# Expert outputs in one PSUM bank instead of two, and a bank of their own for the turned sums of the gathered groups

## The chip, the cores and the metric

One Trainium2 chip, one core of it. The metric is the device time of one launch in microseconds (us), as the median of several runs; lower is better. The engines are TensorE (PE; its weight loads are shown apart as PEld), VectorE (DVE), ScalarE (ACT), GpSimd (POOL) and SyncE (SP, which here only starts DMAs).

## What is computed

Two layers on a tensor x of 4 x 32 x 32 tokens with 128 channels, all in float32. Cut to what matters:

```python
x = x + L0_conv(ln(x))      # deformable convolution: 8 groups of 32 channels, 9 points each,
                            # each point read bilinearly (4 corners) at a place that depends on the token
t = t + L0_ffn(ln(t))       # 8 experts, one per token: y = relu(x @ w1[e] + b1[e]) @ w2[e] + b2[e],
                            # times the probability of the expert, 0 if the expert is over capacity
x = x + L1_conv(ln(x))      # attention in a 7 x 7 window, 8 heads of 16 channels
t = t + L1_ffn(ln(t))       # 8 experts again
```

## The kernel before

The 4096 tokens are 32 tiles of 128. The work on one tile i is a "slot" (function `slot`), in two halves: `beside_second` runs beside the eight experts of the second layer for tile i - 4, `beside_first` beside the eight experts of the first layer for tile i - 1. Each half is one "pass" of `experts`, numbered u. Slots 4 to 22 and 23 to 29 are two hardware loops; slots 0 to 3, 30 and 31 are written out. Behind slot 31 (`final=True`) come five passes (`beside_0` to `beside_4`) that finish the last tiles. There is no scheduler: every engine runs the same order of parts, written by hand, and they wait for one another by semaphores (`Steps`: `step` names what an instruction completes, `done` is the value to wait for).

**Experts.** In a pass, PE multiplies `up(e)` into bank `Z[e % 2]` (L1581, 4 products), ACT makes `hid` of it (L1404), and PE multiplies `down(e)` into `Y[e // 4]` (L1591, 4 products), a quarter bank for each expert. The order on PE is up(e + 1), the early parts of `beside(e)`, down(e), the other parts of `beside(e)`. DVE weights and sums the outputs in `add_up` (L1201): experts 0 to 3 at e = 4, behind `beside(4)` (steps `a0` to `a3`), experts 4 to 7 in `close` (`a4` to `a7`), which stands in `beside(0)` of the next pass; then the rest of `close` adds the result to X. So `down(0)` of a pass waits for `a3` of the pass before, and `down(4)` for `a7` of the pass before. `a0` needs also `share` (the bias part, product L1569, copied by ACT in L1396).

**The convolution.** Six of the eight groups are gathered: POOL starts 54 indirect DMAs for a tile (L894, nine for each group q, into `got[:, q]`), DVE multiplies the weights in (`conv("mix")`, L1130), PE turns and sums the nine points (`conv("gather")`, L1533) and ACT copies the sum to `mixed_T` (L1375). The other two groups are made without a gather: DVE makes 16 masks a tile (`dense("make")`, L1053, called m0 to m15 here), PE turns and sums each (`dense("sum")`, L1490) and ACT copies two at a time to `spread` (L1339). Both kinds of sum go to bank `DGB`: the dense ones to its columns 0 to 255, the gathered ones to columns 256 to 383. The waits keep the engines apart by bank: a gathered sum waits for the copy of the dense ones and of the gathered one before, and a dense sum behind a gathered one for its copy (`freed=mixed`).

POOL writes `got[:, q]` for tile t again when PE has turned it for tile t - 1; in `flow(s)`, s = 0 to 15 of a slot, the parts above are spread over its sixteen experts (`MIXED` says at which s a group is mixed).

Of the kernel before, what the change touches and what calls it, by code (L numbers as in the profile page):

```python
# [36 lines left out]
P = 128  # L37
# [87 lines left out]
def build(nc, x, v_w, v_b, qd_w, qd_b, qs_w, qw_w, qw_b, out_w, out_b, prior, dscale,  # L125
# [3 lines left out]
    with ctx:  # L129
# [6 lines left out]
        def bank(name):  # L136
            return ctx.enter_context(nc.psum_tensor(name, [P, 512], F32))
# [108 lines left out]


        Z = [bank("Z0"), bank("Z1")]
        Y = [bank("Y0"), bank("Y1")]
        N = [bank("N0"), bank("N1")]  # L250
        DGB = bank("DGB")
        CV = bank("CV")
        ALL = [*Z, *Y, *N, DGB, CV]


        x_in = [sem(f"x_in{part}") for part in range(2)]
# [59 lines left out]
        def slots(eng, conv, route, experts, close, qkv, attend, values, places, dense):  # L316


            def slot(i, u1, u0, u0_before, ends, qk, att, e1, val=True, place=True, final=False):
# [4 lines left out]
                at = MIXED if not final else (1, 4, 6, 9, 11, 13)  # L324

                def flow(s):
                    mixed = (conv_s.done(f"c{NQ - 1}", i - 1) if s == 0 else
                             conv_s.done(f"c{at.index(s - 2)}", i) if s - 2 in at else None)
                    if s == 2:
                        dense("apart", i, 1)  # L330
                    if s == 3:
                        dense("now", i, None, i + TB - 1 if val else last)
                    if s == 5:
                        dense("weigh", i, 1)
                    if s == 10 and not final:
                        dense("apart", i + 1, 0)
                    if s == 13 and not final:
                        dense("weigh", i + 1, 0)
                    if s in at:
                        conv("mix", i, at.index(s))  # L340
                    if final and 7 <= s <= 10:
                        dense("make", i, 2 * s - 6)
                        dense("make", i, 2 * s - 5)
                    elif s < 15 and not (final and s > 10):
                        dense("make", i, s + 1)
                    elif not final:
                        dense("make", i + 1, 0)
                    if s - 1 in at:
                        conv("gather", i, at.index(s - 1), (s if s <= 8 else min(16, 2 * s - 8)) if final else s)
                    if final and 8 <= s <= 11:  # L350
                        dense("sum", i, 2 * s - 8, mixed)
                        dense("sum", i, 2 * s - 7)
                        dense("copy", i, s - 4)
                    elif s < 8 or not final:
                        dense("sum", i, s, mixed)
                        if s % 2:
                            dense("copy", i, s // 2)
                    if s - 1 in at:
                        conv("copy", i, at.index(s - 1), (s if s < 8 else min(15, 2 * s - 7)) if final else s)
# [186 lines left out]
            def beside_0(e, early):  # L546
                if early:
# [15 lines left out]
                        route("share", 1, last - 3)  # L563
                    return
                if e == 0:
                    route("pick", 0, last)
                    route("exp", 0, last)
                    close(u - 1, 0, last - 1)
                if e == 1:
                    route("pick", 1, last - 3)  # L570
                    route("exp", 1, last - 3)
# [341 lines left out]
        def _(v):  # L913
# [271 lines left out]
            def add_up(u, n, t, e0, e1):  # L1185

                d, s = exp_v.done, exp_v.step
                gate = route_b[n][:, 5, :]

                v.wait_ge(*exp_t.done(f"y{e1 - 1}", u))  # L1190
                for e in range(e0, e1):
                    so_far = acc
                    if e == 0:

                        v.wait_ge(*route_v[n].done("gate", t))
                        v.wait_ge(*route_s[n].done("b2", t))
                        v.wait_ge(*exp_v.all(u - 1))
                        so_far = share[n]
                    else:
                        v.wait_ge(*d(f"a{e - 1}", u))  # L1200
                    v.scalar_tensor_tensor(out=acc[:, :], in0=Y[e // 4][:, (e % 4) * D:(e % 4 + 1) * D],  # L1201
                                           scalar=gate[:, e:e + 1], in1=so_far[:, :],
                                           op0=ALU.mult, op1=ALU.add).then_inc(*s(f"a{e}"))

            def experts(u, n, t, beside):
                for e in range(E):
                    beside(e, True)
                    beside(e, False)
                    if e == 4:
                        add_up(u, n, t, 0, 4)  # L1210

            def close(u, n, t):
                d, s = exp_v.done, exp_v.step
# [95 lines left out]
        def _(a):  # L1309
# [59 lines left out]
            def conv(part, t, q=None, mine=None):  # L1369
                if part == "copy":  # L1370

                    a.wait_ge(*conv_t.done(f"g{q}", t))
                    a.wait_ge(*dense_t.done(f"k{mine}", t))
                    a.wait_ge(*conv_t.done("proj", t - 1))
                    a.activation(mixed_T[:, q, :], DGB[:, 2 * P:3 * P], ACT.Copy).then_inc(*conv_s.step(f"c{q}"))  # L1375

            def route(part, n, t, freed=None, held=None, placed=None):
                s = route_s[n].step
# [70 lines left out]
        def _(pe):  # L1449
# [29 lines left out]
            def dense(part, t, n=None, freed=None):  # L1479
                if part == "sum":  # L1480
                    pe.wait_ge(*dense_v.done(f"m{n}", t))

                    if n >= 2:
                        pe.wait_ge(*dense_s.done(f"s{n // 2 - 1}", t))
                    else:
                        pe.wait_ge(*dense_s.done("s7", t - 1))
                    if freed is not None:
                        pe.wait_ge(*freed)
                    for k in range(K):
                        ins = pe.matmul(DGB[:, n % 2 * P:(n % 2 + 1) * P], made[:, n % MADE, k * P:(k + 1) * P],  # L1490
                                        ident[:, :], is_transpose=True, start=(k == 0), stop=(k == K - 1))
                    ins.then_inc(*dense_t.step(f"k{n}"))
# [32 lines left out]
            def conv(part, t, q=None, mine=None):  # L1525
                s = conv_t.step
                if part == "gather":
                    pe.wait_ge(*conv_v.done(f"m{q}", t))

                    pe.wait_ge(*(conv_s.done(f"c{q - 1}", t) if q else conv_s.done(f"c{NQ - 1}", t - 1)))  # L1530
                    pe.wait_ge(*(dense_s.done(f"s{mine // 2 - 1}", t) if mine > 1 else dense_s.done("s7", t - 1)))
                    for k in range(K):
                        ins = pe.matmul(DGB[:, 2 * P:3 * P], got[:, q, k * PATCH:(k + 1) * PATCH], ident[:, :],  # L1533
                                        is_transpose=True, start=(k == 0), stop=(k == K - 1))
                    ins.then_inc(*s(f"g{q}"))
                if part == "project":
# [35 lines left out]
            def experts(u, n, t, beside):  # L1572
# [11 lines left out]

                def down(e):
                    pe.wait_ge(*exp_s.done(f"h{e}", u))
                    if e % 4 == 0:

                        pe.wait_ge(*exp_v.done(f"a{e + 3}", u - 1))
                    for c in range(FC):  # L1590
                        ins = pe.matmul(Y[e // 4][:, (e % 4) * D:(e % 4 + 1) * D], hid[:, e % 2, c, :],  # L1591
                                        w2[n][:, e * FC + c, :], start=(c == 0), stop=(c == FC - 1))
                    ins.then_inc(*s(f"y{e}"))

# [124 lines left out]
```

## Time and profile before

| | before |
|---|---|
| time, median of 3 runs | 2698.65 us (2695.47 to 2699.51) |
| time of the profiled execution | 2693.5 us |
| its span, first to last instruction | 2691.7 us |
| PE busy | 2315.7 us (86%) |
| DVE busy | 1912.4 us (71%) |
| ACT busy | 1221.7 us (45%) |
| POOL busy | 1941.1 us (72%) |
| mean granted clock of PE | 0.938 of full speed |

The table says how long an engine worked, not what sets the end. For that one reads the chain that ended last, then the time line of a tile in the loop and that of the end of the program, where POOL has no more gathers.

### The profile page before, as it was taken

How to read it: one execution, taken by the hardware profiler on the slowest of the kernel's cores; microseconds unless marked ns; L12 is line 12 of the kernel's file. 1: busy time of each engine (PE TensorE's matmuls, PEld its weight loads, DVE VectorE, ACT ScalarE, POOL GpSimd, SP SyncE). 2: the span in 40 equal slices, each digit the busy share in tenths (PEclk: the TensorE clock that was granted, in tenths of full speed). 3: DMA queues.
4: the chain of work that ended last, by engine and by line, in shares of the span. 5: the costliest groups of instructions: out<-in, count | busy, mean ns of one | idle time of the engine just before them, and what ended most of it. 6: DMA issues, size and time to landing. Idle time of an engine off the chain costs nothing.

```text
span 2691.7 us, 61285 instructions
## 1 busy us (share of the span) xinstructions
PE 2315.7 (86%) x18976; PEld 2202.2 (82%) x18976; DVE 1912.4 (71%) x4404; ACT 1221.7 (45%) x3974; POOL 1941.1 (72%) x1797
## 2 busy tenths in 40 slices
PE   1477689999988999999999999898988988898988
PEld 1466688988888898888889888888988888898887
DVE  4566677777777777777777777777777777776643
ACT  1123345544544554454455445445544544554455
POOL 3777777777777777777777777777777777777600
PEclk6788899999999999999999999999999999999989
DMA  9512212222221222222122222212111111111100
GB/s 190 140 50 54 60 55 57 57 59 59 60 58 54 57 55 59 59 60 60 54 56 54 59 59 60 60 54 56 48 54 53 54 52 53 49 50 54 49 16 10
DMA packets 219754, 158.70 MB, mean 59 GB/s; under 512 B 149530, under 2 KB 186988, under 8 KB 219596
## 3 DMA queue, kind: packets, MB, share of 16 engines
q0 software_dynamic: 55296, 113.36, 14.8%
q1 hardware_dynamic: 164300, 43.73, 7.4%
q14 instruction: 119, 0.97, 0.1%
q8 instruction: 39, 0.64, 0.1%
HBM read 138.90 MB, written 18.04 MB: 58 GB/s over the span
## 4 chain that ended last, share of the span: by engine, by line
POOL 68%; issue 22%; PE 5%; DVE 1%; ACT 1%; POOLq 1%; SPq 1%; DMA 1%; ACTq 0%; DVEq 0%
POOL got L894 68%; PE Y L1591 1%; PE Z L1581 1%; SPq L760 1%; POOL ranks L886 1%; ACT hid L1404 0%; PE N L1634 0%; PE DGB L1533 0%; PE N L1660 0%; ACT prob L1433 0%; PE N L1652 0%; DMA got<-patches,ranks 0%; PE DGB L1490 0%; DVE made L1053 0%; DVE acc L1201 0%
## 5 line engine op out<-in xcount | busy, mean ns | idle before, releaser
L894 POOL DMA_INDIRECT got<-patches,ranks x1728 | 1925.0, 1114 | 565.7 <-issue 507.8
L1404 ACT ACTIVATE hid<-Z,b 128x128 f32<-128x128 f32 x2048 | 575.3, 371 | 439.4 <-PE Z L1581 439.1
L1053 DVE TENSOR_TENSOR made<-tent 128x1152 f32<-128x1152 f32 x512 | 690.9, 1351 | 9.7 <-PE DGB L1490 9.4
L1490 PE MATMUL DGB<-ident,made 128*128 128x128 f32 x4608 | 611.6, 280 | 54.5 <-DVE bias L1118 39.8
L1591 PE MATMUL Y<-w,hid 128*128 128x128 f32 x4096 | 591.4, 290 | 22.7 <-ACT hid L1404 15.2
L1490 PEld LDWEIGHTS DGB<-ident,made 128*128 128x128 f32 x4608 | 540.1, 146 | 68.8 <-DVE bias L1118 40.6
L1591 PEld LDWEIGHTS Y<-w,hid 128*128 128x128 f32 x4096 | 526.0, 200 | 58.3 <-issue 26.5
L1581 PE MATMUL Z<-xt_m,w 128*128 128x128 f32 x4096 | 536.4, 277 | 0.5 <-ACT xt_m L1386 0.5
L1581 PEld LDWEIGHTS Z<-xt_m,w 128*128 128x128 f32 x4096 | 494.9, 193 | 6.9 <-issue 6.6
L1130 DVE TENSOR_TENSOR got<-got,wq 128x1152 f32<-128x1152 f32 x192 | 260.4, 1356 | 193.1 <-DMA got<-patches,ranks 186.8
L1339 ACT ACTIVATE spread<-DGB 128x256 f32<-128x256 f32 x256 | 97.6, 381 | 463.3 <-PE DGB L1490 460.2
L1533 PE MATMUL DGB<-ident,got 128*128 128x128 f32 x1728 | 251.3, 297 | 25.4 <-DVE got L1130 24.7
L1533 PEld LDWEIGHTS DGB<-ident,got 128*128 128x128 f32 x1728 | 221.0, 155 | 32.1 <-DVE got L1130 27.0
L1201 DVE SCALAR_TENSOR_TENSOR acc<-Y,route,acc 128x128 f32<-128x128 f32 x448 | 156.7, 350 | 76.9 <-issue 57.8
L1565 PE MATMUL CV<-ident,route 128*8 128x128 f32 x128 | 30.8, 333 | 168.5 <-DVE route L1183 168.5
L1565 PEld LDWEIGHTS CV<-ident,route 128*8 128x8 f32 x128 | 6.3, 88 | 182.1 <-DVE route L1183 181.4
L1500 PE MATMUL N<-spread,v_now 128*32 128x128 f32 x1024 | 123.4, 274 | 14.7 <-ACT spread L1339 14.7
L1500 PEld LDWEIGHTS N<-spread,v_now 128*32 128x32 f32 x1024 | 106.4, 110 | 26.5 <-ACT spread L1339 22.5
L1433 ACT ACTIVATE prob<-prob,soft 128x100 f32<-128x100 f32 x256 | 93.2, 373 | 0.0
L1393 ACT ACTIVATE gate_T<-CV 8x128 f32<-8x128 f32 x64 | 16.5, 258 | 156.3 <-PE CV L1565 156.1
L1381 ACT ACT_TABLE_LOAD x62 | 79.5, 1283 | 1.1
L1389 ACT ACT_TABLE_LOAD x61 | 78.3, 1283 | 1.1
(185 smaller groups left out, 2319.8 us busy)
## 6 DMA issues: line engine op xcount, KB each, us to landing
got<-patches,ranks POOLq DMA_INDIRECT x1728
vwin<-vpad SPq DMA_DIRECT2D x320, 40.0 KB
patches<-arena SPq DMA_DIRECT2D x92, 96.0 KB
w<-in_L_ffn_w SPq DMA_DIRECT2D x2, 2048.0 KB
patches<-got SPq DMA_DIRECT2D x38, 96.0 KB, 3.0
vpad<-vt SPq DMA_DIRECT2D x128, 16.0 KB
out<-X SPq DMA_DIRECT2D x32, 64.0 KB, 1.6
X<-in_x SPq DMA_DIRECT2D x1, 576.0 KB, 4.6
```

The costliest lines, as they stand in the source:

```text
L894: pool.indirect_dma_start(out=got[:, q, j * PATCH:(j + 1) * PATCH], out_offset=None, in_=table, in_offset=bass.IndirectOffsetOnAxis(ap=ran ...
L1053: v.tensor_tensor(made[:, n % MADE, :].rearrange("p (k y x) -> p k y x", k=K, y=CHUNK), tent[g][:, 1, :, c * CHUNK:(c + 1) * CHUNK].unsque ...
L1130: v.tensor_tensor(g3, g3, wj.unsqueeze(2).to_broadcast([P, QJ * CORNERS, C]), ALU.mult)\
L1201: v.scalar_tensor_tensor(out=acc[:, :], in0=Y[e // 4][:, (e % 4) * D:(e % 4 + 1) * D], scalar=gate[:, e:e + 1], in1=so_far[:, :], op0=ALU. ...
L1339: a.activation(spread[:, 2 * n:2 * n + 2, :].rearrange("p c q -> p (c q)"), DGB[:, 0:2 * P], ACT.Copy).then_inc(*dense_s.step(f"s{n}"))
L1404: ins = a.activation(hid[:, e % 2, c, :], Z[e % 2][:, c * P:(c + 1) * P], ACT.Relu, bias=b1[n][:, e * FC + c:e * FC + c + 1])
L1433: ins = a.activation(prob[:, j, :], prob[:, j, :], ACT.Exp, bias=soft[:, 1, j:j + 1], accum_out=soft[:, 2, j:j + 1])
L1490: ins = pe.matmul(DGB[:, n % 2 * P:(n % 2 + 1) * P], made[:, n % MADE, k * P:(k + 1) * P], ident[:, :], is_transpose=True, start=(k == 0), ...
L1500: ins = pe.matmul(N[1][n * C:(n + 1) * C, 0:P], v_now[:, c, n * C:(n + 1) * C], spread[:, n * CHUNKS + c, :], start=(c == 0), stop=(c == C ...
L1533: ins = pe.matmul(DGB[:, 2 * P:3 * P], got[:, q, k * PATCH:(k + 1) * PATCH], ident[:, :], is_transpose=True, start=(k == 0), stop=(k == K ...
L1581: ins = pe.matmul(Z[e % 2][:, c * P:(c + 1) * P], w1[n][:, e, c * P:(c + 1) * P], xt_m[n][:, :], start=True, stop=True)
L1591: ins = pe.matmul(Y[e // 4][:, (e % 4) * D:(e % 4 + 1) * D], hid[:, e % 2, c, :], w2[n][:, e * FC + c, :], start=(c == 0), stop=(c == FC - 1))
```

## The change

The outputs of all eight experts share one bank `Y`, in two rounds of four. `down(0)` waits for `a7` of the pass before and the new wait of `down(4)` is for `a3` of its own pass. DVE's first `add_up` of a pass stands ahead of `beside(4)` instead of behind it, and in `beside_0` `close` stands ahead of `pick` and `exp`. The bank that is free becomes `GS`, with a quarter of it for each gathered sum in turn; the waits between the gathered and the dense sums are left out.

```diff
-        Y = [bank("Y0"), bank("Y1")]
+        Y = bank("Y")
+        GS = bank("GS")
...
                 def flow(s):
-                    mixed = (conv_s.done(f"c{NQ - 1}", i - 1) if s == 0 else
-                             conv_s.done(f"c{at.index(s - 2)}", i) if s - 2 in at else None)
...
-                        dense("sum", i, s, mixed)
+                        dense("sum", i, s)
...
                 if e == 0:
+                    close(u - 1, 0, last - 1)
                     route("pick", 0, last)
                     route("exp", 0, last)
-                    close(u - 1, 0, last - 1)
...
-                    v.scalar_tensor_tensor(out=acc[:, :], in0=Y[e // 4][:, (e % 4) * D:(e % 4 + 1) * D],
+                    v.scalar_tensor_tensor(out=acc[:, :], in0=Y[:, (e % 4) * D:(e % 4 + 1) * D],
...
             def experts(u, n, t, beside):
                 for e in range(E):
+                    if e == 4:
+                        add_up(u, n, t, 0, 4)
                     beside(e, True)
                     beside(e, False)
-                    if e == 4:
-                        add_up(u, n, t, 0, 4)
...
                     a.wait_ge(*conv_t.done(f"g{q}", t))
-                    a.wait_ge(*dense_t.done(f"k{mine}", t))
                     a.wait_ge(*conv_t.done("proj", t - 1))
-                    a.activation(mixed_T[:, q, :], DGB[:, 2 * P:3 * P], ACT.Copy).then_inc(*conv_s.step(f"c{q}"))
+                    a.activation(mixed_T[:, q, :], GS[:, q % 4 * P:(q % 4 + 1) * P], ACT.Copy).then_inc(*conv_s.step(f"c{q}"))
...
-                    if freed is not None:
-                        pe.wait_ge(*freed)
...
-                    pe.wait_ge(*(dense_s.done(f"s{mine // 2 - 1}", t) if mine > 1 else dense_s.done("s7", t - 1)))
                     for k in range(K):
-                        ins = pe.matmul(DGB[:, 2 * P:3 * P], got[:, q, k * PATCH:(k + 1) * PATCH], ident[:, :],
+                        ins = pe.matmul(GS[:, q % 4 * P:(q % 4 + 1) * P], got[:, q, k * PATCH:(k + 1) * PATCH], ident[:, :],
...
                 def down(e):
                     pe.wait_ge(*exp_s.done(f"h{e}", u))
-                    if e % 4 == 0:
-
-                        pe.wait_ge(*exp_v.done(f"a{e + 3}", u - 1))
+                    if e == 0:
+                        pe.wait_ge(*exp_v.done("a7", u - 1))
+                    if e == 4:
+                        pe.wait_ge(*exp_v.done("a3", u))
```

On DVE, in the first loop at e = 4 of a slot's first half, there stands before (from m4 on; the first row made is m4, the second m5; `route` holds the gates, and rows of ISA and REGISTER_ALU are waits and addresses):

```order
L1053 TENSOR_TENSOR made<-tent 128x1152
L1130 ISA
L1130 TENSOR_TENSOR got<-got,wq 128x1152
L1049 REGISTER_ALU
L1053 TENSOR_TENSOR made<-tent 128x1152
L1190 ISA
L1195 REGISTER_ALU
L1196 REGISTER_ALU
L1201 SCALAR_TENSOR_TENSOR acc<-Y,route,share 128x128
...
L1160 TENSOR_TENSOR route<-CV,gb 128x8
```

and now, one line number lower:

```order
L1052 TENSOR_TENSOR made<-tent 128x1152
L1189 ISA
L1194 REGISTER_ALU
L1195 REGISTER_ALU
L1200 SCALAR_TENSOR_TENSOR acc<-Y,route,share 128x128
...
L1129 ISA
L1129 TENSOR_TENSOR got<-got,wq 128x1152
L1048 REGISTER_ALU
L1052 TENSOR_TENSOR made<-tent 128x1152
L1158 REGISTER_ALU
L1159 TENSOR_TENSOR route<-CV,gb 128x8
```

The four sums (three of them left out in the rows) have moved ahead of the mix of group 1 and of m5; the rest of the slot keeps its order.

On DVE, at e = 4 of the first pass behind the last slot (`beside_0`), there stands before (QT, KT and vt are the attention's queries, keys and values, `turns` the spread queries):

```order
L1250 TENSOR_SCALAR xn_q<-X,mv_q,rs_q 128x128
L1256 TENSOR_SCALAR QT<-N,bq 128x4x8x4
L1260 TENSOR_SCALAR KT<-N,bq 128x4x32
L1265 TENSOR_TENSOR vt<-N,bv 128x128
L1201 SCALAR_TENSOR_TENSOR acc<-Y,route,share 128x128
L1201 SCALAR_TENSOR_TENSOR acc<-Y,route,acc 128x128 x3
```

and now:

```order
L1249 TENSOR_SCALAR xn_q<-X,mv_q,rs_q 128x128
L1200 SCALAR_TENSOR_TENSOR acc<-Y,route,share 128x128
L1200 SCALAR_TENSOR_TENSOR acc<-Y,route,acc 128x128 x3
L1255 TENSOR_SCALAR QT<-N,bq 128x4x8x4
L1259 TENSOR_SCALAR KT<-N,bq 128x4x32
L1264 TENSOR_TENSOR vt<-N,bv 128x128
```

The sums have moved ahead of the three parts of the attention, and are no longer between these and the spread queries (L1271 before).

## Rows read from the trace of the kernel before

**Rows 1.** The page: POOL in 40 slices of the span; the chain, shares by engine.

```profile
POOL 3777777777777777777777777777777777777600
...
POOL 68%; issue 22%; PE 5%; DVE 1%; ACT 1%; POOLq 1%; SPq 1%; DMA 1%; ACTq 0%; DVEq 0%
```

**Rows 2.** Groups of instructions, one tile of the loop (1183 to 1262 us): busy, mean; idle before.

```profile
L894 POOL DMA_INDIRECT got<-patches,ranks x54 | 60.4, 1118 | 17.7 <-issue 15.9 <-POOL ranks L886 1.8
```

**Rows 3.** Waits over the whole span: total us, times, longest us.

```profile
PE DGB L1490 <- ACT mixed_T L1375: 8.8, 15, 1.6
```

**Rows 4.** Time line of POOL in that tile: start, duration, instruction, idle before.

```profile
1238.15 1.82 POOL L894 DMA_INDIRECT got<-patches,ranks  x1 [0.31 <-issue]
1240.28 0.96 POOL L894 DMA_INDIRECT got<-patches,ranks  x1 [0.30 <-issue]
...
1246.56 1.65 POOL L894 DMA_INDIRECT got<-patches,ranks  x1 [0.30 <-issue]
```

**Rows 5.** Time line of DVE in that tile: a7, m4, mix, pick, m6.

```profile
1222.22 1.51 DVE L1201 SCALAR_TENSOR_TENSOR acc<-Y,route,acc 128x128 f32<-128x128 f32 x4 [3.04 <-issue]
...
1237.80 1.35 DVE L1053 TENSOR_TENSOR made<-tent 128x1152 f32<-128x1152 f32 x1
1239.07 1.35 DVE L1130 TENSOR_TENSOR got<-got,wq 128x1152 f32<-128x1152 f32 x1
...
1243.75 0.17 DVE L1160 TENSOR_TENSOR route<-CV,gb 128x8 f32<-128x8 f32 x1 [0.64 <-PE CV L1556]
...
1246.04 1.35 DVE L1053 TENSOR_TENSOR made<-tent 128x1152 f32<-128x1152 f32 x1
```

**Rows 6.** Time line of PE in that tile: down(0), down(3), down(4), the long wait.

```profile
1224.48 1.15 PE L1591 MATMUL Y<-w,hid 128*128 128x128 f32 x8 [0.39 <-DVE fin L1223]
...
1237.57 1.16 PE L1591 MATMUL Y<-w,hid 128*128 128x128 f32 x8
...
1240.55 1.06 PE L1591 MATMUL Y<-w,hid 128*128 128x128 f32 x8
...
1254.56 0.59 PE L1565 MATMUL CV<-ident,route 128*8 128x128 f32 x2 [4.01 <-DVE route L1183]
```

**Rows 7.** Time line of PE at the end: down(0) and down(4) of slot 31's second pass.

```profile
2519.49 1.16 PE L1591 MATMUL Y<-w,hid 128*128 128x128 f32 x8
...
2537.91 1.06 PE L1591 MATMUL Y<-w,hid 128*128 128x128 f32 x8
```

**Rows 8.** Time line of DVE there: a4 to a7, then a1 to a3.

```profile
2519.80 1.50 DVE L1201 SCALAR_TENSOR_TENSOR acc<-Y,route,acc 128x128 f32<-128x128 f32 x4
...
2539.15 1.12 DVE L1201 SCALAR_TENSOR_TENSOR acc<-Y,route,acc 128x128 f32<-128x128 f32 x3
```

**Rows 9.** Time line of PE, passes one to three and five behind slot 31.

```profile
2570.59 1.16 PE L1591 MATMUL Y<-w,hid 128*128 128x128 f32 x8
...
2576.53 2.67 PE L1634 MATMUL N<-KT,turns 128*128 128x100 f32 x16 [1.88 <-DVE turns L1271]
...
2587.80 1.95 PE L1591 MATMUL Y<-w,hid 128*128 128x128 f32 x8 [2.04 <-ACT hid L1404]
...
2601.86 1.06 PE L1591 MATMUL Y<-w,hid 128*128 128x128 f32 x8
...
2618.58 2.00 PE L1591 MATMUL Y<-w,hid 128*128 128x128 f32 x8 [2.92 <-ACT hid L1404]
...
2680.33 1.06 PE L1591 MATMUL Y<-w,hid 128*128 128x128 f32 x8
```

**Rows 10.** Time line of ACT in pass one: the copy of share.

```profile
2571.30 0.29 ACT L1396 ACTIVATE share<-CV 128x128 f32<-128x128 f32 x1
```

**Rows 11.** Time line of DVE: a4 to a7 in passes two and three, a1 to a3 in pass five.

```profile
2587.75 1.50 DVE L1201 SCALAR_TENSOR_TENSOR acc<-Y,route,acc 128x128 f32<-128x128 f32 x4
...
2618.41 1.50 DVE L1201 SCALAR_TENSOR_TENSOR acc<-Y,route,acc 128x128 f32<-128x128 f32 x4
...
2680.03 1.12 DVE L1201 SCALAR_TENSOR_TENSOR acc<-Y,route,acc 128x128 f32<-128x128 f32 x3
```

More of the change, by code:

```diff
@@ L252, in build @@
         CV = bank("CV")
-        ALL = [*Z, *Y, *N, DGB, CV]
+        ALL = [*Z, Y, GS, *N, DGB, CV]
         x_in = [sem(f"x_in{part}") for part in range(2)]
@@ L350, in flow @@
                     if final and 8 <= s <= 11:
-                        dense("sum", i, 2 * s - 8, mixed)
+                        dense("sum", i, 2 * s - 8)
                         dense("sum", i, 2 * s - 7)
@@ L1586, in down @@
                     pe.wait_ge(*exp_s.done(f"h{e}", u))
-                    if e % 4 == 0:
-                        pe.wait_ge(*exp_v.done(f"a{e + 3}", u - 1))
+                    if e == 0:
+                        pe.wait_ge(*exp_v.done("a7", u - 1))
+                    if e == 4:
+                        pe.wait_ge(*exp_v.done("a3", u))
                     for c in range(FC):
-                        ins = pe.matmul(Y[e // 4][:, (e % 4) * D:(e % 4 + 1) * D], hid[:, e % 2, c, :],
+                        ins = pe.matmul(Y[:, (e % 4) * D:(e % 4 + 1) * D], hid[:, e % 2, c, :],
                                         w2[n][:, e * FC + c, :], start=(c == 0), stop=(c == FC - 1))
```

## The prediction

> **What bounds the kernel now.** I read the page first. The chain that ended last lies on POOL for 68% of the span and in the gaps between its calls for 22%; in the slices POOL works through 38 of 40 and is idle in the last two [rows 1]. The groups of one tile of the loop say what a call costs: 54 calls with 60.4 us busy and 17.7 between them, 78.1 us for a tile, and none of the 17.7 is a wait for PE [rows 2]. PE waits 4.01 us in one place of that tile, for a gate that DVE makes only after it has waited for gathered data [rows 6]: PE has some 4 us to spare in each tile. So in the loop an edit counts only if it makes the 54 calls longer, or costs PE more than that reserve. Behind the gathers, POOL's last two slices, PE, ACT and DVE set the end, and there each new wait of PE counts.
>
> A call is not always the same length: 0.96 us or 1.82 or 1.65 [rows 4]. Laid beside DVE's time line, the long ones started while DVE worked on m4 or m6 (1237.80 to 1239.15 and 1246.04 to 1247.39), and both ended 0.82 us after that product's end [rows 4, 5]. A call that starts under such a mask product is held to its end. The first lost 0.86 us by that, the second 0.69.
>
> **Part 1, the sums in a bank of their own.** It removes waits between PE and ACT and adds no instruction: the same products and copies, other columns. The largest of these waits as the trace names them, of PE for a copy to mixed_T, is 8.8 us in the whole span, 15 times [rows 3]. Most of it lies before POOL's end, inside the reserve. Taken as 0; bounds 0 and -1 us.
>
> **Part 2, one Y bank, in the loop.** down(0) now waits for a7 of the pass before. In the tile shown a7 is done at 1222.22 + 1.51 = 1223.73 and down(0) starts at 1224.48 [rows 5, 6]: 0.75 us to spare, no wait. down(4) waits for a3 of its own pass. The output of expert 3 is there at 1237.57 + 1.16 = 1238.73, DVE is free behind m4 at 1239.07, four sums take 1.5 us: a3 at 1240.57, and down(4) started at 1240.55 [rows 5, 6, 11]. PE thus waits some 0.05 us, and I allow as much again for weights that are not loaded ahead. The logits behind it and DVE's pick, which already waits for them (0.64 us), come that much later, m6 too, and with m6 the end of the call held under it. That is 0.1 us a tile on POOL's own time, for 32 tiles +3 us. Bounds: 0, if the wait stays hidden, and +6 with as much in the tile's other pass.
>
> **Part 3, the moved sums.** The mix of group 1 and m5 start 1.5 us later and fill time in which DVE waited for the logits: 1240.57 + 2 x 1.27 = 1243.1, before 1243.75 [rows 5]. (1.27 is the distance from m4 to the mix.) Which call is held changes. The call at 1240.28 no longer meets the mix; the one 1.25 us later starts at 1241.5 under it and is held to 1241.8, some 0.25 us; every later call shifts by that, so the call under m6 starts 0.25 later and is held 0.25 less, 0.45 in place of 0.69. The sum for the tile stays: 0. Had one call more or less fitted between m4 and m6, it would be another sum (below).
>
> The Trainium skill, "SBUF — State Buffer", section "Who interferes with whom", says that a tensor_tensor has no two-port mode, contends only with GpSimd's reads and did not stall the writing of descriptors. The calls of [rows 4] beside [rows 5] speak against this for indirect DMAs. By the page a moved mask product costs nothing; by the rows it could, and comes to nothing only by the sum above.
>
> **Part 4, the end of the program.** Here a wait of PE isn't hidden, step by step:
> - Slot 31, second pass. a7 is done at 2519.80 + 1.50 = 2521.3, but down(0) started at 2519.49 [rows 7, 8]: 1.85 us of wait. down(4) started at 2537.91; a3 comes at 2539.15 + 1.12 = 2540.3, since DVE's mix ahead of it waits for gathered data. With the first wait PE comes at 2539.8, so the two together make 2.4 us, not 4.3. Behind a wait of 2 us PE is slow for a while: eight products took 1.95 us behind a wait of 2.04, and 1.06 elsewhere [rows 9]. I add 0.9: +3.3 (2.4 to 5).
> - Pass one. a0 needs share, copied at 2571.30 + 0.29 [rows 10]; a3 at 2573.1, down(4) at 2570.59 [rows 9]: 2.5 us. The sums (1.5) are then out of the way of the spread queries, for which PE waited 1.88 us at 2576.53: +1.0 (0 to 2.5). Moving close ahead of pick there costs nothing: DVE does both before PE asks again.
> - Pass two. a7 at 2587.75 + 1.50 = 2589.3, down(0) at 2587.80 [rows 9, 11]: +1.5, although it already waited 2.04 for hid. down(4), at 2601.86, may wait too, but frees DVE as in pass one: 0.
> - Pass three. a7 at 2618.41 + 1.50 = 2619.9, down(0) at 2618.58: +1.4 [rows 9, 11].
> - Passes four and five have nothing else beside them by then. In five a3 is done at 2680.03 + 1.12 = 2681.15, and down(4) started at 2680.33 [rows 9, 11]: +0.85, and as much for four: +1.7.
> Together 8.9 us, bounds 5 and 14.
>
> **The sum.** 3 + 8.9 = +12 us, on the profiled execution's 2693.5: 2705.5. That execution lies 5.1 us below the median, 2698.65; on the median it is 2710.5. What a measurement of this kernel tells from no change is 0.2%, 5.4 us.
>
> **The rivals.**
> *Hidden after all (no change).* For it: the passes at the end hold waits of 1.88 to 2.92 us for ACT and DVE [rows 9], and a later down(0) may only shorten the next of them. Against it: down(0) of passes two and three stands behind such a wait already, not ahead of it. It gives half of part 4 or less and nothing in the loop, +3 us: 2702.
> *Dearer waits in the loop (slower still).* down(4) has no reserve at all in the loop (0.02 us late), and what stands behind it on PE are the logits that DVE's pick waits for. If the wait costs 0.7 us a tile rather than 0.1, it is 32 x 0.6 = +19 more: 2730. It decides where a3 comes more than 0.5 us behind PE, for instance if the mask products of both passes are late. DVE's free time ahead of the sums speaks against it.
> *The calls fall better (faster).* The time lost under m6 is 0.69 us in each tile [rows 4]. If m6 starts 0.5 us later against the calls, the call at 1246.56 is started before it and isn't held: 0.7 us a tile, 32 x 0.7 = 22 less, 2688.5. It decides at that half microsecond; I count a shift of 0.1 to 0.35 for m6 against the calls. The other masks of a tile may cross such a line as well, in either direction.
>
> **How the numbers follow.** The forecast (slower by 6 to 20 us) has 0.58, hidden 0.20, dearer waits 0.13, better calls 0.09. The time is that of the first, 2710.5. For the range I take the bounds of parts 2 and 4 (+5 to +20, 2703.5 to 2718.5) and reach down into the hidden case and up into the dearer one: 2698 to 2725. Its lower end leaves out the faster case, the upper one half of the dearer. Faster by over 0.2%: 0.10 (the better calls, and a little of the hidden case). Within 0.2%: 0.19. Slower: 0.71.
>
> **What would show it.** Right: 54 calls of a tile still take 78.1 to 78.3 us; down(4) starts some 0.1 us behind a3 in the loop; in the last 180 us PE waits for the sums in down(0) or down(4) of every pass, 8 to 10 us more in all; no DGB product waits for mixed_T. Wrong: the tile's time moved by half a microsecond or more either way (then the calls under masks m4 to m6 are other ones), or the waits at the end appear but the last product isn't later by their sum.

## The result and the profile after

The change made the kernel slower: 2716.01 us (median of 5 runs, 2711.65 to 2716.76) against 2699.51 (5 runs, 2695.47 to 2703.99), ratio 1.0055 with the interval 1.0040 to 1.0071. The profiled execution took 2714.46 us (span 2712.7), 21.0 more than that of before. The forecast was 2710.5.

Waits of PE after the change, between POOL's last gather and the end (total us, times, longest):

```profile
PE Y L1587 <- DVE acc L1200: 14.6, 8, 4.1
PE Y L1587 <- ACT hid L1402: 3.8, 4, 3.0
PE N L1630 <- DVE turns L1270: 1.9, 3, 0.9
```

The first line is new: eight waits of down(0) or down(4) for the sums. The time line of PE shows most of them one by one. The first two rows are slot 31's second pass [rows 7], which lies ahead of POOL's end, so they come on top of the eight. Then come down(4) of pass one, both of pass two, down(0) of pass three, down(4) of pass four and down(0) of pass five [rows 9]. Left out are down(0) of pass four, 0.50 us, and down(4) of pass five, 0.80 us:

```profile
2532.71 1.13 PE L1587 MATMUL Y<-w,hid 128*128 128x128 f32 x8 [1.90 <-DVE acc L1200]
...
2552.00 1.13 PE L1587 MATMUL Y<-w,hid 128*128 128x128 f32 x8 [0.72 <-DVE acc L1200]
...
2587.84 1.13 PE L1587 MATMUL Y<-w,hid 128*128 128x128 f32 x8 [2.80 <-DVE acc L1200]
2592.80 2.03 PE L1630 MATMUL N<-KT,turns 128*128 128x100 f32 x16 [0.93 <-DVE turns L1270]
...
2604.19 2.05 PE L1587 MATMUL Y<-w,hid 128*128 128x128 f32 x8 [3.73 <-DVE acc L1200]
...
2620.38 1.13 PE L1587 MATMUL Y<-w,hid 128*128 128x128 f32 x8 [0.69 <-DVE acc L1200]
...
2635.64 2.04 PE L1587 MATMUL Y<-w,hid 128*128 128x128 f32 x8 [4.08 <-DVE acc L1200]
...
2682.40 1.13 PE L1587 MATMUL Y<-w,hid 128*128 128x128 f32 x8 [1.09 <-DVE acc L1200]
...
2691.46 1.13 PE L1587 MATMUL Y<-w,hid 128*128 128x128 f32 x8 [0.86 <-DVE acc L1200]
```

What they wait for, in pass one: ACT's copy of share [rows 10], then DVE's sums, in the time lines of ACT and of DVE:

```profile
2585.68 0.29 ACT L1394 ACTIVATE share<-CV 128x128 f32<-128x128 f32 x1
```

```profile
2586.18 0.35 DVE L1200 SCALAR_TENSOR_TENSOR acc<-Y,route,share 128x128 f32<-128x128 f32 x1 [4.25 <-ACT share L1394]
2586.57 1.12 DVE L1200 SCALAR_TENSOR_TENSOR acc<-Y,route,acc 128x128 f32<-128x128 f32 x3
```

The sums end at 2587.69, down(4) starts at 2587.84. The time lines of the same tile of the loop as in [rows 4 to 6]: PE's down(4), then m4, the sums, the mix, m5, pick and m6 on DVE, then POOL's calls.

```profile
1249.62 1.16 PE L1587 MATMUL Y<-w,hid 128*128 128x128 f32 x8
```

```profile
1246.79 1.35 DVE L1052 TENSOR_TENSOR made<-tent 128x1152 f32<-128x1152 f32 x1
...
1248.44 1.12 DVE L1200 SCALAR_TENSOR_TENSOR acc<-Y,route,acc 128x128 f32<-128x128 f32 x3
1249.48 1.35 DVE L1129 TENSOR_TENSOR got<-got,wq 128x1152 f32<-128x1152 f32 x1
1250.75 1.35 DVE L1052 TENSOR_TENSOR made<-tent 128x1152 f32<-128x1152 f32 x1
1252.92 0.17 DVE L1159 TENSOR_TENSOR route<-CV,gb 128x8 f32<-128x8 f32 x1 [0.83 <-PE CV L1551]
...
1255.22 1.35 DVE L1052 TENSOR_TENSOR made<-tent 128x1152 f32<-128x1152 f32 x1
```

```profile
1247.14 1.82 POOL L893 DMA_INDIRECT got<-patches,ranks  x1 [0.30 <-issue]
1249.27 0.95 POOL L893 DMA_INDIRECT got<-patches,ranks  x1 [0.31 <-issue]
1250.52 1.13 POOL L893 DMA_INDIRECT got<-patches,ranks  x1 [0.30 <-issue]
...
1255.73 1.66 POOL L893 DMA_INDIRECT got<-patches,ranks  x1 [0.30 <-issue]
```

a3 is done at 1249.56 and down(4) starts 0.06 later. pick comes 6.13 us behind m4 (before 5.95) and m6 8.43 (before 8.24), each 0.2 us later where I had costed 0.1. The call at 1250.52 is held under the mix by 0.19 (forecast 0.25); the one under m6 still loses 0.72, since m6 moved as much as the calls did. The groups of POOL over a tile say what came of it:

```profile
L893 POOL DMA_INDIRECT got<-patches,ranks x54 | 60.5, 1119 | 17.6 <-issue 15.9 <-POOL ranks L885 1.8
```

That is the tile of [rows 2], 78.1 us in both kernels. The waits of the DGB products for mixed_T [rows 3] are gone.

**Where the time went.** I cut each profiled execution into five stages, at the start of POOL's 325th gather (tile 6) and of its first for tile 31, at the end of its last and at the start of down(7) of slot 31's second pass. The last stage is the "five passes". All times are us, counted from the first instruction; the table already holds the experiments below. (Two expectations below give the start of tile 6 as 505.4 and 514.5, counted from 0.3 us earlier; here these are 505.1 and 514.2.)

| kernel | tile 6 starts | tile 6 to 31 | calls of tile 31 | to down(7) | five passes |
|---|---|---|---|---|---|
| before | 505.1 | 1964.5 | 76.3 | 9.0 | 136.8 |
| before, again | 508.7 | 1964.6 | 76.8 | 8.1 | 132.3 |
| order alone | 511.0 | 1965.2 | 78.2 | 9.4 | 132.4 |
| two banks at the end | 510.0 | 1966.4 | 78.5 | 12.9 | 131.9 |
| first wait alone | 508.6 | 1963.4 | 77.9 | 11.9 | 135.8 |
| second wait alone | 510.1 | 1964.0 | 76.3 | 11.6 | 135.7 |
| after | 514.2 | 1964.1 | 79.2 | 11.6 | 143.6 |
| after, again | 508.9 | 1966.2 | 78.5 | 12.9 | 144.0 |
| sums in DGB | 506.7 | 1966.6 | 78.5 | 12.9 | 144.0 |
| filled waits | 511.4 | 1966.7 | 78.6 | 12.9 | 137.8 |

### The profile page after: what moved, and what is told of

Read it like the earlier page. It is cut to its first block, busy times and chain, and to the rows that moved or that the text cites. A ratio compares the mean times of both kernels' runs of the same rounds, so it can differ in the third digit from the quotient of the medians.

```text
span 2712.7 us, 61024 instructions
## 1 busy us (share of the span) xinstructions
PE 2329.8 (86%) x18976; PEld 2206.2 (81%) x18976; DVE 1913.2 (71%) x4404; ACT 1220.8 (45%) x3974; POOL 1953.2 (72%) x1797
## 4 chain that ended last, share of the span: by engine, by line
POOL 66%; issue 22%; PE 5%; SPq 3%; DVE 2%; ACT 1%; POOLq 1%; DMA 1%; ACTq 0%; DVEq 0%
POOL got L893 65%; SPq L782 2%; PE Y L1587 1%; PE Z L1576 1%; SPq L759 1%; DVE acc L1200 1%; PE DGB L1486 1%; DVE made L1052 1%; POOL ranks L885 1%; SPq L788 0%; PE GS L1528 0%; DVE got L1129 0%; PE N L1656 0%; ACT prob L1431 0%; PE N L1630 0%
## 5 line engine op out<-in xcount | busy, mean ns | idle before, releaser
L1587 PE MATMUL Y<-w,hid 128*128 128x128 f32 x4096 | 598.3, 292 | 36.8 <-DVE acc L1200 20.4
L1528 PE MATMUL GS<-ident,got 128*128 128x128 f32 x1728 | 253.8, 299 | 26.9 <-DVE got L1129 26.9
L1528 PEld LDWEIGHTS GS<-ident,got 128*128 128x128 f32 x1728 | 222.5, 156 | 33.8 <-DVE got L1129 29.8
L1200 DVE SCALAR_TENSOR_TENSOR acc<-Y,route,acc 128x128 f32<-128x128 f32 x448 | 156.9, 350 | 76.8 <-issue 56.6
L1299 DVE COPY turns<-N 128x512 f32<-128x512 f32 x32 | 22.1, 692 | 115.3 <-PE N L1648 115.3
```

Of the source, the lines that this page charges most:

```text
L1200: v.scalar_tensor_tensor(out=acc[:, :], in0=Y[:, (e % 4) * D:(e % 4 + 1) * D], scalar=gate[:, e:e + 1], in1=so_far[:, :], op0=ALU.mult, op ...
L1528: ins = pe.matmul(GS[:, q % 4 * P:(q % 4 + 1) * P], got[:, q, k * PATCH:(k + 1) * PATCH], ident[:, :], is_transpose=True, start=(k == 0), ...
L1587: ins = pe.matmul(Y[:, (e % 4) * D:(e % 4 + 1) * D], hid[:, e % 2, c, :], w2[n][:, e * FC + c, :], start=(c == 0), stop=(c == FC - 1))
```

## The experiments

Each ratio below is against runs of the kernel before that were made beside it on the same chip; their median is given.

**The same two kernels again.** The first 9 us of the 21 lay ahead of tile 6, where I had forecast nothing.

> The kernel before, unchanged. In the first comparison the gather of tile 6 started 9.1 us later after the change than before (514.5 against 505.4 us), and stayed that much later to tile 31; the rest of the 21.0 us between the two profiled spans lies behind the start of tile 31. Theory C (the start is chance: whether a GpSimd call meets a long VectorE product there differs from execution to execution): this execution starts tile 6 at another place than 505.4, by several us, and its span moves with it. Theories A and B (the start is due to the change): tile 6 within 1 us of 505.4, span 2691 to 2693.

> The changed kernel, unchanged. Theory C: tile 6 starts at another place than 514.5 us, by several us. Theories A and B: within 1 us of it, span 2712 to 2714. By either, from the start of tile 31 to the end it takes the same 234 us as in the first profile of it.

Measured: before 2696.40 us, ratio to the runs beside it (2694.37, 23 runs) 1.0007 (0.9997 to 1.0018); after 2714.29 (4 runs), ratio 1.0086 (1.0064 to 1.0108). Tile 6 starts at 508.7 and 508.9 us. So theory C holds: the 9 us ahead of tile 6 are chance, and the pair profiled first lay at the two ends of it. From the start of tile 31 the end takes 235 us again.

**Where the gathered sums stand.** The edit takes the first part of the change back:

```
-   pe.matmul(GS[:, q % 4 * P:(q % 4 + 1) * P], got[:, q, ...], ...)
+   pe.matmul(DGB[:, 2 * P:3 * P], got[:, q, ...], ...)          # and all old waits
```

> One bank for the expert outputs, with the new order on VectorE and the new waits, but the gathered sums stay in the bank of the dense ones, with the old waits. Theory A (the 9 us at the start come from the waits that were left out, since VectorE's products then lie closer together under the calls): tile 6 starts near 505, and the time is some 2706, the kernel before + 7 to 8 (the cost behind tile 31 stays, or is 1 us more). Theory B (they come from the new place of the sums on VectorE): tile 6 near 514, time near that of the changed kernel, 2716. Theory C (chance): tile 6 anywhere from 505 to 515.

Measured: 2710.01 us, ratio 1.0062 (1.0047 to 1.0077), against the same runs as the two above. The intervals of this one and of after overlap, from tile 31 on every stage has the length of after, again, the five passes the same 144.0 us, and tile 6 starts at 506.7, inside the scatter. That is 15.6 us above before where theory A had 7 to 8. Theories A and B fall; the bank of its own is worth nothing that these runs can tell.

**The order alone.** Before, with DVE's order of after (not printed: `close` ahead of `pick` in `beside_0`):

```
             for e in range(E):
+                if e == 4:
+                    add_up(u, n, t, 0, 4)
                 beside(e, True)
                 beside(e, False)
-                if e == 4:
-                    add_up(u, n, t, 0, 4)
```

> The kernel before with only VectorE's new order (the first four sums ahead of beside(4), close ahead of pick in the first pass behind the last slot); two banks for the outputs and all old waits stay. Behind the start of tile 31 every theory expects no wait of TensorE for the sums, so 0 to 2 us less than the kernel before there (the sums are earlier out of the way of the spread queries). Theory A: tile 6 near 505, time within 2 us of the kernel before. Theory B: tile 6 near 514, time + 7 to 9. In the loop the tile takes 78.4 to 78.6 us as in both kernels; if it is the shifted products that were to cost in the loop, they would show here, too.

Measured: 2691.98 us (12 runs, 2684.95 to 2698.94), ratio 0.9991 (0.9979 to 1.0004). No loss in the loop. PE's waits for the spread queries behind POOL's end, before and then with the order alone:

```profile
PE N L1634 <- DVE turns L1271: 4.2, 3, 1.9
```

```profile
PE N L1634 <- DVE turns L1271: 2.2, 3, 1.2
```

They fell by 2 us, which is the part that was to come back. So the loss comes with the bank and its waits, not with the order.

**One wait at a time.** The order of after, two Y banks, and only one of the waits:

```
     # first wait alone                          # second wait alone
     if e in (0, 4): wait a7 of u - 1            if e == 0: wait a3 of u - 1
                                                 if e == 4: wait a3 of u
```

> The kernel before with the new order on VectorE, two banks for the outputs and one of the new waits alone: down(0) waits for a7 of the pass before (down(4) too, which is no new wait). With the order alone it took 141.8 us from GpSimd's last call to the end. Theory W (each wait costs its idle time and some slow clock behind it): down(0) waits for the sums some 1.9 us in slot 31 and 1.7, 1.2, 0.2 and 0.5 us longer than before in the passes behind it; 145 to 148 us from the last call to the end, the time + 4 to 8 on the order alone, 2696 to 2700. Rival (hidden after all): within 2 us of the order alone, since the next wait shrinks by as much.

> As the run before, but with the other wait alone: down(4) waits for a3 of its own pass (down(0) for a3 of the pass before, as ever). Theory W: down(4) waits 0.7 us in slot 31, then 2.8, 0.7, 0, 1.1 and 0.8 us in the five passes; in the first two some 2.5 us come back at the spread queries, so 143 to 147 us from the last call to the end, time + 2 to 5 on the order alone. The two waits together are then the 13 to 15 us of the changed kernel, unless the clock loses more when both are there. In the loop neither wait shows: tile 6 to tile 31 takes 1964 to 1967 us in both runs.

Measured (before beside them 2695.12, 28 runs): 2701.42, ratio 1.0025 (1.0016 to 1.0034), and 2701.18, ratio 1.0024 (1.0014 to 1.0034). From POOL's last call to the end it took 147.7 us, inside its 145 to 148, and 147.4, just above its 143 to 147. down(4) of slot 31 waited 2.20 us in the second run, where 0.7 were expected, since no late down(0) stands ahead of it there. The stretch of the five passes, as length, PE busy (instructions), granted clock, DMA share and GB/s, in this order for: before, before again, order alone, first wait, second wait, after, after again.

```profile
2554.94:2691.70 136.76, 115.44 (x893) 0.93 0.05 13
```

```profile
2558.21:2690.50 132.29, 110.94 (x893) 0.97 0.05 13
```

```profile
2563.86:2696.30 132.44, 113.84 (x893) 0.94 0.05 13
```

```profile
2561.80:2697.60 135.80, 113.47 (x893) 0.95 0.05 13
```

```profile
2562.10:2697.80 135.70, 112.25 (x893) 0.95 0.05 13
```

```profile
2569.11:2712.70 143.59, 116.38 (x893) 0.92 0.04 12
```

```profile
2566.44:2710.40 143.96, 116.99 (x893) 0.92 0.04 12
```

All have the same 893 instructions. Length less busy is the time in which PE stood: 21.3 and 21.4 before, 18.6 with the order alone, 22.3 and 23.5 with one wait, 27.2 and 27.0 with both. The idle time adds up (3.7 + 4.9 = 8.6; measured 8.6 and 8.4). The busy time doesn't: 112.3 to 113.8 us with the order alone or one wait, 116.4 and 117.0 with both, for the same products. The granted clock, 0.92 in place of 0.94 and 0.95, goes with it. Against before, each wait alone lies 8 to 9 us above the order alone, dearer than expected (4 to 8 and 2 to 5); 3.4 of it are in the five passes, about 2.4 in slot 31, and the rest I can't place.

**Two banks where they are free.** After the last gathered sum GS stands empty. In the five passes experts 0 to 3 go there. In short (down(0) of the first of the five waits for ACT's copy of the last gathered sum instead):

```
+   late = isinstance(u, int) and u >= 2 * NT - 5
+   bank = GS if late and e < 4 else Y
+   down(0): wait a3 of u - 1,  down(4): wait a7 of u - 1     # if late
```

> The changed kernel, but in the five passes behind the last slot experts 0 to 3 go to the bank GS, which has no gathered sums any more, and experts 4 to 7 to Y, so that the waits of down(0) and down(4) are again those on the pass before. From the end of GpSimd's last call to the end of the span it took 145.8 and 140.4 us before, 155.2 and 156.8 after the change. Theory W (that difference is the shared bank in these passes, by idle time and by the lower clock behind it): 141 to 146 us, and the time 8 to 13 us less than the changed kernel, near 2703. Rival (it comes from the moved sums, or from the wait in slot 31 that makes everything behind it late): 153 us or more, time unchanged within 3 us.

Measured: 2703.97 us, ratio 1.0038 (1.0024 to 1.0053). The five passes:

```profile
2567.87:2699.80 131.93, 113.56 (x893) 0.94 0.05 13
```

The end behind POOL's last call takes 144.8 us. Theory W holds: in these five passes the shared bank costs 12 us against this trace (143.6 and 144.0 against 131.9), and 9.3 against the mean of the two traces of before, which lie 4.5 us apart. Against before this kernel still loses 8.9 us in the median. The stages show 4.3 in slot 31 and 1.9 each in the loop and in tile 31, less 2.6 in the five passes, 5.5 in all.

**Is it clock or idle time?** PE is kept at work in three of the new waits:

```
+   extra = {(59, 4): 10, (60, 0): 12, (61, 0): 14}.get((u, e), 0)   # passes one to three
+   for c in range(extra):       # ahead of down(e); nobody reads GS any more
+       pe.matmul(GS[...], w1[n][:, e, ...], xt_m[n][:, :], start=True, stop=True)
```

> The changed kernel, with TensorE kept at work in its three longest new waits by products that nobody reads (10 before down(4) of pass one, 12 and 14 before down(0) of passes two and three, some 0.27 us each, a little less than the waits of 2.8, 3.7 and 4.1 us). They change no wait for the sums, only what TensorE does meanwhile. In the changed kernel the end behind GpSimd's last call took 155.2 and 156.8 us, with a mean granted clock of 0.92 and TensorE 127 to 129 us busy; the kernel before had 0.94 and 0.97, 118 to 124 us busy. Theory K (some 5 to 7 us of the 13 are clock, lost behind the waits): the clock rises to 0.95 or more, the end takes 149 to 153 us, the time falls by 3 to 7 us. Rival (the slow clock comes with the other waits, before and behind these, or the idle time itself is all of the cost): 155 to 158 us and an unchanged clock.

Measured: 2708.82 us, ratio 1.0048 (1.0034 to 1.0063) to before, 2697.14 (11 runs). The stretches of 10 us behind down(0) of pass two, down(0) of pass three and down(6) of pass three, first after, then with filled waits:

```profile
2604.20:2614.20 10.00, 10.00 (x63) 0.69 0.01 2
2635.60:2645.60 10.00, 9.96 (x64) 0.73 0.03 8
2661.00:2671.00 10.00, 9.42 (x67) 0.83 0.01 2
```

```profile
2604.60:2614.60 10.00, 9.99 (x86) 1.00 0.00 0
2633.10:2643.10 10.00, 9.99 (x84) 1.00 0.12 36
2658.50:2668.50 10.00, 9.50 (x81) 0.98 0.03 8
```

A clock of 0.69 over a stretch is a mean of full speed, 2.4 GHz, and the lower level, 1.2 GHz. With the waits filled PE gets through 86 instructions in the first stretch where it did 63. The five passes, with 72 instructions more:

```profile
2569.53:2707.30 137.77, 118.81 (x965) 0.97 0.05 13
```

The end behind POOL's last call falls to 150.6 us, inside theory K's 149 to 153, and the five passes from 144.0 to 137.8. The first filled wait ends where it did, 31.6 us behind POOL's last call here and in after, again; only what stands behind it comes sooner, down(0) of pass two by 2.6 us. So 6 us of the tail are clock. This rests on the traces (three with the waits unfilled at 143.6 to 144.0, one with them filled): the median lies 5 to 8 us nearer to before than those of after, but the interval of its ratio overlaps that of the first comparison (1.0040 to 1.0071).

**Halves, and quarters.** The calls that are held cost 9.6 us in each tile, more than anything in this change. Here the mask products and the mixes are cut in two or four along their free size, in the kernel before:

```
+   for h in range(2):
+       ins = v.tensor_tensor(m4[:, :, h * half:(h + 1) * half, :], ...)   # mixes likewise
+   ins.then_inc(*dense_v.step(f"m{n}"))
```

> The kernel before, with each of VectorE's 16 mask products and 6 mixes of a tile (128x1152) made by two instructions of 128x576. Theory H (a GpSimd call that starts under such a product is held to that instruction's end): the calls get through between the halves, the time lost in a tile's 54 calls falls from 9.6 us to some 5, and the tile from 78.5 us to 74 to 75, where TensorE, with some 4 us to spare in a tile, becomes the bound; in all 2580 to 2610 us. Rival 1 (the call waits until VectorE pauses, or for a fixed time): the loss stays near 9.6 us a tile and the time near 2695. Rival 2 (the second instructions' own overhead on VectorE costs more than it brings): over 2700.

> The kernel before, with VectorE's mask products and mixes made by four instructions of 128x288 each. Theory H (a call is held to the end of the instruction under which it starts): the loss is some 2.5 us a tile, GpSimd would need 71.4 us for a tile and TensorE, busy 68.5 us of it at full clock, is the bound with its waits: a tile of 72 to 73.5 us, in all 2510 to 2550. Rival (a call is let in only in a gap of VectorE, which short back-to-back instructions don't leave, or the added instructions cost as much as they bring): 2570 or more.

Measured: halves 2577.90 us, ratio 0.9555 (0.9540 to 0.9570); quarters 2586.27, ratio 0.9594 (0.9567 to 0.9621). For halves theory H holds, with a time 2 us below its 2580 to 2610. A stretch of the time lines with halves, DVE and then POOL:

```profile
1188.08 1.42 DVE L1056 TENSOR_TENSOR made<-tent 128x576 f32<-128x576 f32 x2
```

```profile
1187.27 1.04 POOL L894 DMA_INDIRECT got<-patches,ranks  x1 [0.30 <-issue]
1188.61 1.03 POOL L894 DMA_INDIRECT got<-patches,ranks  x1 [0.30 <-issue]
```

A half takes 0.75 us (the mean of its line), so the first ends at 1188.83 and the second at 1189.50. The call at 1188.61 ends at 1189.64, 0.81 behind the first. The tile took 74.7 us on average, 5.7 of it loss; PE still waits in each tile, so it is near to being the bound, but not yet the bound that the expectation made it. For quarters theory H gave 2510 to 2550, and that failed. The time lines of DVE and POOL say why:

```profile
979.78 0.82 DVE L1136 TENSOR_TENSOR got<-got,wq 128x288 f32<-128x288 f32 x2
980.52 1.56 DVE L1055 TENSOR_TENSOR made<-tent 128x288 f32<-128x288 f32 x4
```

```profile
980.05 2.84 POOL L894 DMA_INDIRECT got<-patches,ranks  x1 [0.30 <-issue]
```

This call was held until 0.81 us behind the last of six instructions, not of one. It started under the first of the six. In the trace with quarters the loss is 5.8 us a tile, as with halves, where I had 2.5. Between 500 and 2300 us 31 calls went past the end of their quarter in this way; what they lost by it is 2.1 of the 5.8. The time lies in the rival's range, but most calls were let in between two quarters (last section), so its first reason fails as a rule.

**The change with halves.** TensorE's spare time in a tile shrinks with the tile, so a wait hidden in the loop might show.

> The changed kernel with two banks in the last five passes and with VectorE's products in halves. If the cost of the shared bank lies where the first runs had it (behind GpSimd's last call, and 2 us in tile 31), this is the kernel before with halves (2577.9 us) + 3 to 9: 2581 to 2587. Theory U (in the loop TensorE has only some 2.5 us to spare in a tile now, so the wait of down(4) for a3 shows there, 0.1 to 0.5 us a tile): 2586 to 2600. Theory P (the waits that were left out pay now that TensorE is nearly the bound): under 2577.

> The changed kernel with VectorE's products in halves and nothing else. Its distance to the run with two banks at the end is the price of the shared bank in the last five passes, which was 10 us: so 2591 to 2597 by the first theory, 2596 to 2610 by theory U, under 2588 by theory P.

Measured: 2584.43, ratio 0.9576 (0.9561 to 0.9591), and 2593.98, ratio 0.9621 (0.9605 to 0.9637); before beside them 2698.64 (9 runs). Both medians fall in the ranges of the first theory. The distance, 9.6 us, is what the shared bank costs in the five passes, where the traces have 141.0 against 133.8; it is rough, since the five runs of each are spread over 21 and 11 us. Theory U has ranges that begin only 2 us higher, so the times alone don't rule it out, but the loop does: tile 6 to 31 took 1865.0 and 1858.8 us in these two and 1867.9 in before with halves, though in after with halves down(0) as well as down(4) now starts some 0.06 us behind the sums. Theory P falls by the times. Whether the loop's 3 and 9 us less are scatter or something that the change gives there, one trace of each can't tell. The lowest median of all is that of before with halves; its interval just meets the one of two banks at the end with halves.

## Why the prediction came out right, and where it was not

**Part 1, sums in a bank of their own: 0.** Right, by the run with the sums in DGB: its stages differ from after, again by 0.4 us at most behind tile 6.

**Part 2, the wait in the loop: +3.** The mechanism is as written (down(4) 0.06 us behind a3, pick and m6 0.2 later), but its size is smaller: tile 6 to 31 takes 1964.6 us before and 1964.1, 1966.2 and 1966.6 with the shared bank, 1 us more on average and not distinct from scatter. Both traces of after show the same 0.06 us in both passes of nearly every tile, where I had it in one of the two. PE stands for it 0.31 us in the second pass of slots 23 to 29 and 1.0 us in that of slot 30, 3.2 us in all, and its reserve takes that up.

**Part 3, the moved sums: 0.** Right for the loop, with one error inside: the call under m6 was to be held 0.25 us less, and lost 0.72 as before, since m6 moved with the calls. In tile 31 the calls took 76.3 and 76.8 us before and 78.5 to 79.2 in all kernels with the shared bank in slot 31, 2 us that I did not forecast. POOL waits for nothing new there, it is the length of the calls. The runs with the order alone or one wait gave 78.2, 77.9 and 76.3, so which edit does it stays open.

**Part 4, slot 31: +3.3.** Measured as the distance from POOL's last call to down(7): 8.6 us before (two traces), 12.5 after (three), +3.9. down(0) waited 1.90 us, forecast 1.85 (the rows named there give 1.81), and down(4) 0.72 behind it.

**Part 4, the five passes: +5.6.** PE stood 5.7 us longer (27.1 against 21.4). Pass by pass in the first pair: one, a wait of 2.80 us (forecast 2.5), of which 0.95 came back at the spread queries (1.88 became 0.93) and 0.75 in two waits for hid ahead of it that are gone (+1.1, forecast 1.0); two, 3.73 in place of 2.04 and a new 0.69, of which 1.42 came back at its spread queries (1.66 became 0.24; +1.0, forecast 1.5); three, 4.08 in place of 2.92 (+1.2, forecast 1.4); four and five, two waits each where I had one, 0.50 and 0.86 in place of 0.34 each, 1.09 and 0.80 new (together +2.6, forecast 1.7). So the idle time was forecast well. **The step that was mis-sized** is the clock behind the waits. I gave it 0.9 us once, in slot 31. In the five passes the same 893 instructions kept PE busy for 116.8 us (mean of three) against 113.2 (mean of two), +3.6, and filling the waits gave 6 us back. [Rows 9] had the sign of it, the eight products that took 1.95 us behind a wait of 2.04; I read it as the price of one down, where it is the beginning of a slow stretch. Before has such stretches too, and not in each execution: in the 10 us from that down on, PE got through 71 instructions at a granted clock of 0.83 in the first trace and 86 at 1.00 in the second, behind a wait of 2.13. Over the five passes that is 0.93 and 0.97, and it is its whole scatter of 4.5 us in this stage, since PE stood for 21.3 and 21.4 us. The 3.6 us is thus a difference of means of which one has a wide spread; the filled waits, and not these means, show that clock is lost.

**The sum.** 1 (loop) + 2 (tile 31) + 3.9 + 9.3 = 16 us, and the medians differ by 16.5 and 19.9. The forecast of 12 had 2 too much in the loop and 6 too little behind it: the errors, opposite in sign, made the number look better than its parts. To that extent it was luck. Of its signs, the tile's 78.1 us and the waits came as written: PE stood 8.3 us longer (1.90 and 0.72 in slot 31, 5.7 behind it), inside the 8 to 10. But the end came later than by their sum, by 13.2 us counted from POOL's last call, and the prediction had named that as a sign of being wrong: what lies between is mostly the clock. The profiled pair's 21.0 holds another 9 us ahead of tile 6 that the repeated traces show to be chance.

**The rivals.** "Hidden after all" fell: where a longer wait for the sums stood ahead of one for turns, it shrank that one, and two short ones for hid went, but the other waits absorbed nothing. "Dearer waits in the loop" fell, even where TensorE had less to spare. "The calls fall better" did not happen.

## What to carry to other kernels

Before sharing a buffer, list each place where the producer comes round to it, and look at the end of the program apart from the loop: the same wait was at most 0.31 us in the two hardware loops, and hidden, and up to 4.1 at the end. A wait of TensorE costs its idle time and can cost slower products behind it; where it couldn't be removed, harmless products in it gave two thirds of the loss in these passes back. And a cost per call that one sees in passing, 9.6 us in each tile, gave 117 us when the products that hold the calls were cut in two, six to seven times what the change under study cost.

## What the runs showed of the hardware

GpSimd's indirect DMA calls (0.94 us otherwise) are held by VectorE's mask products and mixes, whose two inputs lie in SBUF. Between 500 and 2300 us of the kernel before, 319 of 1237 calls started under one with over 0.15 us of it to go, and every one ended 0.81 to 0.85 us behind its end; the 275 that started while VectorE stood took 0.94 us on average and 0.97 at most. Not held, at 0.94 us on average, were 105 calls under sums that read PSUM and one SBUF tile, 17 under a product that reads PSUM (`prob<-N,bias`) and 20 under a copy out of PSUM. Two inputs in SBUF don't make it certain: of ten calls under the product that weights `tent`, the five that started in its first 0.04 us were not held, and the product took 0.51 to 0.53 us in place of 0.45. With halves it was so for 11 calls that started in the first 0.03 us of one (0.80 to 0.82 us in place of 0.75), with quarters for 7.

The Trainium skill, "SBUF — State Buffer", section "Who interferes with whom", lets a tensor_tensor with both inputs in SBUF contend with a GpSimd instruction that reads SBUF, and infers that the writing of descriptors isn't stalled by it. These calls take their offsets from an SBUF tile (`ranks`), so by its first half they may be held, and the prediction's reading that by the page a moved mask product costs nothing leaves that out. The traces show that the calls are held, and cutting the products in two took 4.5% off the kernel; which part of a call is held, its reading of offsets or its writing of descriptors, no run here separates. The sums that read PSUM, and held none, agree with the page.

Back to back short products don't always let a call in at their next boundary. With quarters 431 calls started under one with over 0.15 us of it to go: 393 ended within 0.05 us of 0.82 us behind it, 7 weren't held, and 31 went past one boundary or more, 28 of them to 0.82 us behind the last of the run. All 31 had started 0.25 to 0.29 us into their quarter, where 52 others were let in at its end. What decides between the two was not found.

GpSimd's own copies are held too, and in the written-out slots at the start for longer. POOL's copy of ranks ahead of tile 1, before and after:

```profile
112.77 0.52 POOL L886 COPY ranks<-rank 128x36 uint32 x1
```

```profile
112.00 4.58 POOL L885 COPY ranks<-rank 128x36 uint32 x1
```

In that time VectorE ran four mask products and mixes one behind another, to 116.50, and the copy ended at 116.58. Of the 9 us by which the first two profiles differ at tile 6 this is the largest single piece, and it is chance: in the repeated runs the copy took 4.58 us in the kernel before and not in the changed one.
